# A graph network kernel on one core: the first two quarters of the products earlier in a round, and the last stage inside layer 2's rounds

## What is computed

```python
def attention(h, a_src, a_dst, src, dst):        # one layer, per head
    alpha = leaky_relu(a_src[src] + a_dst[dst], 0.2)
    e = exp(alpha - segment_max(alpha, dst)[dst])
    return segment_sum(e * h[src], dst) / segment_sum(e, dst)

h1  = relu(attention(x @ W1, ...) + b1)              # layer 0: H = 4, with self-loops
y   = layernorm(x + attention(h1 @ W2, ...) + b2)    # layer 1: H = 4, with self-loops
h   = y @ W_lin + b_lin
out = leaky_relu(attention(h @ W_gat, ...) + gat_bias, 0.01)   # layer 2: H = 8
result = layernorm(h + out)
```

## Time and profile before

| | |
|---|---|
| Profiled execution, own time | 6752.08 us |
| Its span in the trace | 6750.3 us |
| Granted TensorE clock, mean | 0.767 |
| TensorE matmuls busy | 4987.2 us (74%) |
| TensorE weight loads busy | 3760.2 us (56%) |
| VectorE busy | 4543.9 us (67%) |
| ScalarE busy | 2986.8 us (44%) |
| GpSimd busy | 4612.2 us (68%) |
| DMA, mean | 152 GB/s |

### The profile page before, as it was taken

One profiled execution on the slowest core, in us unless ns is written; L12 is line 12 of the kernel. 1 busy time (PEld: TensorE's weight loads), 2 busy tenths in 40 slices (PEclk: granted clock), 3 DMA queues, 4 the chain that ended last, 5 costly groups with the idle time before them and its releaser, 6 DMA issues. The chain is left out here.

```text
span 6750.3 us, 105201 instructions
## 1 busy us (share of the span) xinstructions
PE 4987.2 (74%) x21652; PEld 3760.2 (56%) x21653; DVE 4543.9 (67%) x13212; ACT 2986.8 (44%) x4940; POOL 4612.2 (68%) x4838
## 2 busy tenths in 40 slices
PE   6777777777777577777777777757777777777776
PEld 5555555555555455555555555535555555555553
DVE  6666666666666667777777777766666666666668
ACT  3344444444344245555555555534344444333435
POOL 2777777777777477777777777737777777777754
PEclk8777777777777677877777777767778777777777
DMA  7555555555555355555555555535555555555545
GB/s 266 144 150 147 148 147 145 149 148 148 147 146 149 98 149 157 159 159 159 157 160 156 158 160 158 155 109 154 152 151 154 153 152 150 150 152 153 154 126 153
DMA packets 505818, 1026.49 MB, mean 152 GB/s; under 512 B 146891, under 2 KB 313199, under 8 KB 504878
## 3 DMA queue, kind: packets, MB, share of 16 engines
q0 software_dynamic: 226208, 633.50, 35.1%
q1 hardware_dynamic: 278798, 382.44, 17.5%
HBM read 931.37 MB, written 84.15 MB: 150 GB/s over the span
## 5 line engine op out<-in xcount | busy, mean ns | idle before, releaser
L1036 POOL DMA_INDIRECT e_rows<-table,loaded x4689 | 4515.6, 963 | 1960.9 <-issue 1694.8
L1293 PE MATMUL e_p_mm<-e_rows,e_onehot 128*128 128x264 f32 x9378 | 2851.9, 467 | 10.5 <-DVE e_rows L1477 7.5
L1293 PEld LDWEIGHTS e_p_mm<-e_rows,e_onehot 128*128 128x128 f32 x9378 | 2177.1, 237 | 493.0 <-issue 11.6
L1477 DVE TENSOR_TENSOR e_rows<-e_rows,e_p_pair 128x1024 f32<-128x1024 f32 x1173 | 1414.0, 1205 | 0.0
L1705 DVE TENSOR_TENSOR_SCAN e_fwd<-e_mask,e_p_one 64x128 f32<-64x128 bf16 (+1 forms) x294 | 121.8, 414 | 1797.1 <-PE e_p_one L1376 1795.3
L1469 DVE TENSOR_TENSOR e_onehot<-e_col,e_p_pair 128x512 f32<-128x512 f32 (+1 forms) x1176 | 903.3, 768 | 79.5 <-issue 75.2
L1301 PE MATMUL e_p_one<-ad_parts,e_onehotT 128*128 x5586 | 707.6, 189 | 154.7 <-issue 146.0
L1301 PEld LDWEIGHTS e_p_one<-ad_parts,e_onehotT 128*128 128x128 bf16 x5586 | 555.7, 103 | 331.7 <-issue 203.8
L1155 ACT ACTIVATE e_onehotT<-e_onehotT,minus_pidx 128x2432 bf16<-128x2432 bf16 x294 | 681.6, 2319 | 42.2 <-DMA e_pass<-pass_rows 41.8
L1158 ACT ACTIVATE e_onehotT<-e_onehotT,one_col 128x2432 bf16<-128x2432 bf16 x294 | 682.7, 2322 | 9.6
L1388 PE MATMUL e_p_small<-ident,e_fwd 64*1 64x64 f32 (+1 forms) x294 | 77.0, 262 | 588.2 <-issue 580.8
(11 more groups left out here) (327 smaller groups left out, 6006.6 us busy)
## 6 DMA issues: line engine op xcount, KB each, us to landing
e_onehotT<-rel_rows SPq DMA_DIRECT2D x294, 608.0 KB
e_rows<-table,loaded POOLq DMA_INDIRECT x4689
e_own_row<-table SPq DMA_DIRECT2D x196, 128.0 KB, 3.1
table<-e_rows_out SPq DMA_DIRECT2D x98, 132.0 KB, 2.0
table<-n_rows_out SPq DMA_DIRECT2D x14, 910.0 KB, 15.5
table<-e_rows_out SPq DMA_DIRECT2D x98, 130.0 KB, 2.6
n_inputs<-in_x_turned SPq DMA_DIRECT2D x14, 896.0 KB, 11.5
e_mask<-mask_rows SPq DMA_DIRECT2D x196, 64.0 KB
```

What stands on the lines that cost most here:

```text
L1036: pool.indirect_dma_start(rows[k][:, g, 0:TW], None, table[L], bass.IndirectOffsetOnAxis(ap=idx[k][:, g:g + 1], axis=0)).then_inc(s_gat[k] ...
L1293: ins = nc.tensor.matmul(p_mm[:, bass.ds(region, MW)], onehot[:, g, :], rows[k][:, g, :], start=False, stop=True, skip_group_check=True)
L1477: return nc.vector.tensor_tensor(feats, feats, p_e[:, gs, :].unsqueeze(3).to_broadcast([P, n, H, C]), ALU.mult)
```

## The change

1. **TensorE's body.** The words `offs`, `flag` and `slots` are read ahead of the wait for `compact`; `old_slots` is read behind `products(2)`. The wait for `cleared` and `products(0)` stand between the lookups and `colsum`, `products(1)` between `colsum` and `topT`.
2. **ScalarE's body.** `prepare_sums` stands ahead of `lookup_rows`.
3. **Roots.** The inverse root is exp(-0.5 ln(v + eps)), two activations from a table that is loaded at the start of the layer; the reciprocal on VectorE goes.
4. **The last stage.** `final_phase` and `resid` go. In layer 2 block w - 5 is finished in round w: `last_sums` in the place of `add_linear`, a relu (`above_zero`) into its own buffer, `last_blocks` and `last_shift` on VectorE, `last_rows` on ScalarE, `last_blocks` and `store_block` on SyncE. A tail of about nine short rounds on each engine follows the last round, with the merge in it. `b_lin + 0.01 * gat_bias` is made in the input phase. There is one `vin`, one `part` and one PSUM tile `p_node`; `summed` is there twice.
5. All layers have twelve rounds written out ahead of the loop.

```diff
@@ TensorE, body @@
                     if not first:
                         regions = words(pe, REGION_ROW, (w - 1) * G, G, (REGIONS - 1) * BANK)
-                        old_slots = words(pe, WINDOW_ROW, (w - 1) * WIN + W_TILE, EXTRAS, G - 1)
+                    offs = words(pe, AD_ROW, w * G, G, (PLACES - 1) * ADS_W)
+                    flag, *extra_ad = words(pe, WINDOW_ROW, w * WIN + W_FLAG, 1 + EXTRAS, (PLACES - 1) * ADS_W)
+                    slots = words(pe, WINDOW_ROW, w * WIN + W_TILE, EXTRAS, G - 1)
...
-                    if LINEAR:
-                        add_linear(w, past)
+                    if LINEAR and finished(w, 5):
+                        last_sums(w, u, i)
                     if CARRY and finished(w, 7):
                         multiply(w, u)
-                    offs = words(pe, AD_ROW, w * G, G, (PLACES - 1) * ADS_W)
-                    flag, *extra_ad = words(pe, WINDOW_ROW, w * WIN + W_FLAG, 1 + EXTRAS, (PLACES - 1) * ADS_W)
-                    slots = words(pe, WINDOW_ROW, w * WIN + W_TILE, EXTRAS, G - 1)
...
                     last.then_inc(st["lookup"], 1)
+                    if not first:
+                        wait_apart(pe, st["cleared"], past)
+                    products(0)
                     wait_apart(pe, st["carry"], now)
                     for o, src in ((COLS_AT, outf), (COLS_AT + 1, outb)):
                         last = nc.tensor.transpose(p_small[0:HG, o:o + 1], flat(src), ident[0:1, 0:1])
                     last.then_inc(st["colsum"], 1)
-                    if not first:
-                        wait_apart(pe, st["cleared"], past)
+                    products(1)
                     wait_apart(pe, st["top"], now)
                     nc.tensor.transpose(p_top[:, 0:HG], seg[:], ident[0:HG, 0:HG]).then_inc(st["topT"], 1)
-                    products(0)
-                    products(1)
...
                     products(2)
+                    if not first:
+                        old_slots = words(pe, WINDOW_ROW, (w - 1) * WIN + W_TILE, EXTRAS, G - 1)
@@ TensorE, layer 2 @@
-                def add_linear(w, past):
-
-                    wait_apart(pe, st["kept"], past)
-                    wait_apart(pe, s_turned, count(pe, w * 16 + 16))
+                def last_sums(w, u, i):
+
+                    r = (u - 5) % TURNS
+                    wait_apart(pe, s["v1"], place_of(pe, w, 5))
+                    if finished(w, 6):
+                        wait_apart(pe, s["value"], place_of(pe, w, 6))
+                    nc.tensor.matmul(p_node[:, 0:D], one_parts, bias2_parts, start=True, stop=False)
+                    nc.tensor.matmul(p_node[:, 0:D], ident[:], vin[:], start=False, stop=True)
+                    pe.wait_ge(s_rst[r], count(pe, pair_of(u, i, 5) * 16))
+                    nc.tensor.matmul(p_node[:, D:2 * D], one_parts, lin_parts, start=True, stop=False)
                     for c in range(2):
-                        nc.tensor.matmul(p_node[:, 0:D], turned[:, c, :], lin[:, c, :], start=c == 0, stop=False)
-                    nc.tensor.matmul(p_node[:, 0:D], one_parts, lin_parts, start=False, stop=True).then_inc(st["linear"], 1)
+                        nc.tensor.matmul(p_node[:, D:2 * D], turned[:, c, :], lin[:, c, :], start=False, stop=False)
+                    nc.tensor.matmul(p_node[:, D:2 * D], slope_ident, vin[:], start=False, stop=True).then_inc(s["mm"], 1)
@@ ScalarE @@
+                nc.scalar.preload_act_table_set("natural_log_exp_and_others")
...
-                    nc.scalar.activation(root[:, r:r + 1], mv[:, r, 1:2], ACT.Sqrt, bias=eps_col[:, 0:1]).then_inc(s["root"], 1)
+                    nc.scalar.activation(root[:, r:r + 1], mv[:, r, 1:2], ACT.Ln, bias=eps_col[:, 0:1]).then_inc(s["root"], 1)
+                    act.wait_ge(s["root"], j)
+                    nc.scalar.activation(rinv[:, r:r + 1], root[:, r:r + 1], ACT.Exp, scale=-0.5).then_inc(s["rinv"], 1)
...
+                def above_zero(w, u, i):
+
+                    act.wait_ge(s["mm"], place_of(act, w, 5))
+                    if finished(w, 6):
+                        act.wait_ge(s["value"], place_of(act, w, 6))
+                    nc.scalar.activation(part, p_node[:, 0:D], ACT.Relu, scale=1.0 - OUT_SLOPE).then_inc(s["part"], 1)
+
+                def last_rows(w, u, i):
+
+                    r = (u - 6) % TURNS
+                    act.wait_ge(s["shift"], place_of(act, w, 6))
+                    nc.scalar.activation(summed[r][:], summed[r][:], ACT.Identity, bias=shift[:, r:r + 1], scale=rinv[:, r:r + 1]
+                                         ).then_inc(s["node"], 1)
...
-                    if LINEAR:
-                        act.wait_ge(st["linear"], now)
-                        if not first:
-                            act.wait_ge(s_linout, count(act, w * 16))
-                        nc.scalar.copy(summed[:], p_node[:, 0:D]).then_inc(st["kept"], 1)
+                    if LINEAR and finished(w, 6):
+                        inverse_roots(place_of(act, w, 6), (u - 6) % TURNS)
                     if NORMED and finished(w, 6):
                         roots(place_of(act, w, 6), (u - 6) % TURNS)
+                    if not first:
+                        prepare_sums(old, past)
+                    if LINEAR and finished(w, 5):
+                        above_zero(w, u, i)
                     if not (isinstance(w, int) and w == WINDOWS - 1):
                         lookup_rows((u + 1) % TURNS, used(u, i, TURNS, -1), count(act, now + 1))
-                    if not first:
-                        prepare_sums(old, past)
                     if CARRY:
                         carried(w, u, i)
+                    elif finished(w, 6):
+                        last_rows(w, u, i)
@@ VectorE, layer 2, behind the fourth quarter @@
+                def last_blocks(w, u, i):
...
+                    if finished(w, 5):
...
+                        dve.wait_ge(s["part"], j)
+                        nc.vector.tensor_tensor(summed[r][:], p_node[:, D:2 * D], part, ALU.add).then_inc(s["value"], 1)
...
+                        nc.vector.bn_stats(stats[:], summed[r][:]).then_inc(s["stats"], 1)
...
+                        nc.vector.bn_aggr(mv[:, r, :], stats[:]).then_inc(s["mean"], 1)
+                    if finished(w, 4):
...
+                        nc.vector.tensor_tensor(vin[:].rearrange("p (h c) -> p h c", h=H), num,
+                                                share[:, (u - 5) % BUFS, :].unsqueeze(2).to_broadcast([P, H, C]), ALU.mult
+                                                ).then_inc(s["v1"], 1)
@@ SyncE, layer 2 @@
-                    if LINEAR and not (isinstance(w, int) and w < 2):
-                        store_summed(w - 2, ago(2))
-                        load_turned(w - 1)
...
+                        last_blocks(w, u, i)
...
+                    if LINEAR:
+                        store_block(w, u)
```

277 lines of the change are left out of this document (93 added, 184 removed).

## The result

The changed kernel takes 6536.7 us (median of 4 runs, 6526.1 to 6552.4) beside 6753.4 us of the kernel before (4 runs, 6746.1 to 6760.1): a ratio of 0.968, 95% interval 0.966 to 0.970. The forecast was 6691 us with a range of 6540 to 6840, so the time lies just under the range, and the gain of 217 us is three and a half times the 61 us that were forecast. The profiled execution took 6552.4 us, its span is 6550.3 us, at a mean granted clock of 0.838. Most of the experiments' chips took 9570 to 10420 us for every kernel that ran there; times are compared within one chip only, and where a reading needs a chip of the kind above, the text says so.

What follows compares the result with a forecast made beforehand. The prediction took TensorE's own loop to bind, with GpSimd just behind. From 6752.1 us it added 58 for rounds, -2 for Ln and Exp, 1 for layer start and -118 for the last stage: 6691 us, range 6540 to 6840.

Steps and rivals of the forecast that it cites:

- What binds now: Rounds: TensorE's own loop binds, GpSimd just behind; `extras` waits 2.75 us in TensorE's queue after VectorE's fourth message.
- `srcT` to the fourth message without a stall: Each round, from `srcT` through VectorE's chain: 13.2 us in layers 0 and 1, 14.1 us in layer 2.
- Fourth message to next `srcT`: Each round's head: issues 1.0 us, loads of words 4.5, waits 0.5, together 6.0 us, no longer hidden by a backlog.
- the back edge: TensorE's loop branch of 4.04 us once in six rounds: 0.7 us a round, 0.6 in layer 2.
- S: VectorE's stall for `colsum` behind `products(0)` in layers 0 and 1: 1.4 us a round, possible range 0 to 2.5.
- S': The same VectorE stall for `colsum` in layer 2, new sums ahead: 1.4 us a round, possible range 0 to 4.0.
- The sum for `colsum`: Layer 2, TensorE's work from `srcT` through `colsum`, added in series: 8.05 or 12.0 us by clock; VectorE wants it at 8.0.
- The last stage: After the last `extras`: 155.8 us go, a tail of five blocks and merge takes 38, so -118 us.
- Ln and Exp: Roots in layer 1: two table loads of 1.283 us a round go, mostly hidden; -2 us behind its last round.
- Rival 1: Products fill TensorE's gaps, the clock stays up, S near 0, S' 0.3: 6447 us, or half, 6540; chance 0.18.
- Rival 2: Loop of `srcT`, VectorE and words slower, `colsum` at half clock, S and S' 2: 6868 us; chance 0.27.
- what would have shown the forecast wrong: Idle before `srcT` still for `compact`, granted clock well over 0.77, or layer 2's round not longer than layer 0's.

Runs made afterwards that it cites:

- e12: The changed kernel with VectorE's reduction and SyncE's one-hot load waiting for `colsum` instead of the lookups' signal: 6572.4 us, ratio 0.975 to the kernel before.
- e13: e12 with the products with `vin` left out of layer 2's `last_sums`: 6592.1 us, ratio 0.979 to the kernel before.
- e2: The changed kernel with multiply's two f32 matmuls done twice in layers 0 and 1: 10171.1 us beside 10306.1 for the kernel before, ratio 0.986.

## Why the prediction missed

- **What binds now, right.** `extras` follows the fourth message by 0.15 us in all layers instead of 2.7 to 3.6.
- **`srcT` to the fourth message without a stall, right.** 13.2 and 14.1 us were taken; before it is 13.14, 13.31 and 14.25 in the table.
- **Fourth message to next `srcT`, right.** In rounds where `srcT` comes over 0.75 us after `compact`, so where the words decide, it is 5.98, 6.17 and 5.96 us (medians); 6.0 was the term; its parts, the estimate of 0.14 us an issue among them, were not measured one by one. The means of 6.6 to 6.7 are the forecast's 6.6 to 6.7 with the back edge.
- **S in layers 0 and 1, right in size, in part by luck.** Taken 1.4; measured 14.55 - 13.14 = 1.41 and 14.62 - 13.31 = 1.31, and VectorE's wait for `colsum` in layer 0 is 135.5/98 = 1.4 us. But 1.4 stood for a clock between the two levels (`products(0)` at 2.7 us) and lookups at their full 3.5 us with the row turns. `products(0)` took 3.8 in every round, and row turns with lookups 4.52 - 1.85 = 2.7: one term was 1.1 us too small, the other 0.8 too large. Rounds of 21.3 were forecast; 21.10 and 21.27 came; against the 0 and -20 us of the sum the layers gained 21 and 25.
- **S' in layer 2, the step that failed.** Taken 1.4, measured 14.30 - 14.25 = 0.05; VectorE waits 11.1 us for `colsum` in the whole layer. The round is 20.99 us instead of 22.1, and the layer gained 30.8 us where the sum had it lose 78: 109 of the 154 us by which the forecast was too high. The sum for `colsum` put the new sums (2.3 us), the row turns (0.3) and the lookups (3.2 us) one behind the other. Put the measured times of the other terms into it: row turns at 3.40, then 0.3 + 3.2, `products(0)` 2.21, `colsum` 0.35 make 9.5 us, again 1.4 more than the 8.05 at which S' was 0. So sums and clock came about as S' = 1.4 had them, and the miss is the term of the lookups.

  Row turns and lookups took 4.90 - 3.40 = 1.5 us instead of 3.5. Of the difference 0.3 was counted twice: the 3.2 us were read from 5539.97, where the row turns start. The other 1.7 were not TensorE's work. Where TensorE is free, its sequencer sets the lookups' pace, 1.90/16 = 0.12 us each; where the sums keep it busy and no load of words is in the way, half of them are issued meanwhile (nine of 16 in the round shown), and the 16 take 1.06 us. So from layer 0 to layer 2 the row turns come 1.55 us later, but the lookups' end only 0.38; from e12 to e13 and in e2, where the work in front was changed alone, the same shows.

  In the Trainium skill, TensorE: Matmul & The Clock Gate, section "Architectural detail: the array is 16× 32×32, not 1× 128×128", TensorE's queue is 64 instructions deep, which fits lookups that wait ready behind the sums; no run here shows the depth.
- **The last stage, right in sum.** 118 us forecast, 119 measured. The five blocks take 4.6 to 6.5 us each instead of 5.6, most of them at half clock.
- **Ln and Exp, not seen.** The 2 us were to come behind layer 1's last round, and the gap between layers 1 and 2 is 87.1 us instead of 87.0. The gap between layers 0 and 1, which has no root ahead of it, fell from 72.4 to 70.5 us; that the sum comes out is luck, and what shortened it is not shown.
- **The rest.** The median lies 15.7 us under the profiled execution that the sum was made for; before they were equal.
- **Rival 1** gave layer 2 a round of 21.0 us, and its half, 6540, the time. Its mechanism holds in layer 2's `products(0)`, at full clock in 92% of the rounds, and fails in layers 0 and 1, at half clock in all. The number is luck: half of the rival's gain is -0.35, -0.45 and -0.15 us a round in the three layers, and -0.22, -0.26 and -0.32 came. It was given 0.18, on the ground that the lookups stay in front; the work that the change itself adds in front of layer 2's lookups was counted as cost and not as what closes the gap.
- **Rival 2** had the right loop, and priced it too high. GpSimd's wait for `extras` fell from 41.7 to 18.1 us in layer 0, but only from 84.9 to 79.0 in layer 1 and from 86.4 to 62.9 in layer 2.

Of what would have shown the forecast wrong, two came true: the clock rose to 0.84, and layer 2's round is not the longest but the shortest. A third came true in part: in 143 of 294 rounds TensorE still waits for `compact` before `srcT`.

## What to carry to other kernels

Before adding up one engine's work in front of a signal, ask of each term whether the engine or its sequencer sets its pace: terms of the two kinds overlap, and work added ahead of small, issue-bound matmuls can be free. That needs the sequencer to be free at that time: here the loads of words had to go ahead first. Work that closes a gap can also buy clock for what follows it, so removing it can cost time. And once the chains inside a round fit, look at the loop's back edge: in this kernel, writing out the loop with its 42 branches of 4.2 us was worth some 150 us, more than the last stage was.
